# Where the jump of a loop falls: VectorE's loop body rotated in a two-layer graph attention kernel

## What is computed

```python
# layer 0: masked attention, residual, layer norm
q, k, v = heads(x @ Wq + bq), heads(x @ Wk + bk), heads(x @ Wv + bv)
attn = softmax(where(adj == 0, -inf, q @ k.T / sqrt(32)))
x = layernorm((attn @ v) @ Wo + bo + x) * gamma + beta
# layer 1: pre-norm attention with an edge bias, then an MLP
nx = layernorm(x) * g1 + b1
bias = where(adj > 0, 0.1 * adj * adj, -inf)
x1 = x + softmax(q(nx) @ k(nx).T / sqrt(32) + bias) @ v(nx) @ wo + bo
return x1 + gelu((layernorm(x1) * g2 + b2) @ w1 + c1) @ w2 + c2
```

## Time and profile before

| | |
|---|---|
| median of 3 runs | 2272.08 us (2271.01 to 2278.83) |
| profiled execution | 2272.97 us, span 2271.2 us |
| TensorE busy | 2150.3 us, 95% |
| VectorE busy | 1827.5 us, 80% |
| ScalarE busy | 1821.7 us, 80% |
| GpSimd busy | 1238.3 us, 55% |
| DMA, data / code | 10.4% / 0.4% of 16 engines |
| granted TensorE clock, mean | 0.988 |

### The profile page before, as it was taken

The page is one execution under the profiler, slowest core; times in us unless marked ns, Lnnn a source line. Parts: engine busy times, 40 slices in busy tenths (PEclk is TensorE's granted clock), DMA queues, the critical chain, the costliest instruction groups (busy, mean ns, idle before and its releaser), DMA issues.

```text
span 2271.2 us, 59215 instructions
## 1 busy us (share of the span) xinstructions
PE 2150.3 (95%) x19008; PEld 1894.4 (83%) x19008; DVE 1827.5 (80%) x7173; ACT 1821.7 (80%) x5774; POOL 1238.3 (55%) x909
## 2 busy tenths in 40 slices
PE   6889999999999999999999999999999999999997
PEld 5678888888888888888888888888888888888886
DVE  5788888888877888878888878888788887788863
ACT  4688888888788887878888878887788887888863
POOL 2566556556556556455566455565455565565541
PEclk8999999999999999999999999999999999999998
DMA  4101110101110101100101100101101111100000
GB/s 128 38 20 39 34 39 16 38 28 37 33 38 14 38 28 38 33 26 26 38 28 38 33 24 28 38 28 38 33 14 38 30 36 33 38 14 28 25 11 19
DMA packets 80891, 73.79 MB, mean 32 GB/s; under 512 B 3008, under 2 KB 72256, under 8 KB 80704
## 3 DMA queue, kind: packets, MB, share of 16 engines
q1 hardware_dynamic: 80704, 71.98, 10.4%
HBM read 55.20 MB, written 16.78 MB: 32 GB/s over the span
## 4 chain that ended last, share of the span: by engine, by line
PE 76%; DVE 9%; ACT 8%; issue 5%; POOL 1%; DMA 0%; DVEq 0%; SPq 0%; ACTq 0%; POOLq 0%
PE ps L402 56%; PE ps L384 9%; PE ps L371 6%; ACT pm L521 5%; PE ps L395 4%; DVE actl L738 2%; DVE pm L698 2%; PE ps L413 1%; DVE r L798 1%; DVE hf L751 1%; ACT acth L570 1%; ACT pt L529 1%; ACT acth L580 1%; DVE stats L783 1%; POOL pm L857 0%
## 5 line engine op out<-in xcount | busy, mean ns | idle before, releaser
L521 ACT ACTIVATE pm<-pm,nmax 128x128 f32<-128x128 f32 x2048 | 794.9, 395 | 86.4 <-DVE nmax L698 85.9
L857 POOL TENSOR_TENSOR pm<-pm,rinv 128x512 f32<-128x512 f32 x512 | 526.3, 1044 | 359.4 <-DVE rinv L713 359.4
L698 DVE CUSTOM_DVE_ANT_0 pm<-ps,m 128x128 f32<-128x128 f32 x2048 | 465.7, 284 | 26.8 <-PE ps L384 22.3
L521 ACT ACTIVATION_READ_ACCUMULATOR pm<-pm,nmax 128x1 f32 x2048 | 396.0, 193 | 0.0
L872 POOL TENSOR_TENSOR rstd<-veps,power 128x4 f32<-128x4 f32 x96 | 98.1, 1022 | 479.1 <-DVE veps L791 479.0
L384 PE MATMUL ps<-ident,pm 128*128 128x128 f32 x2048 | 301.2, 278 | 8.7 <-POOL pm L857 7.5
L402 PE MATMUL ps<-w2h,hh 128*128 128x256 f32 x1024 | 289.9, 283 | 3.2 <-DVE hl L805 3.2
L402 PE MATMUL ps<-w2l,hh 128*128 128x256 f32 x1024 | 287.1, 280 | 0.0
L402 PE MATMUL ps<-w2h,hl 128*128 128x256 f32 x1024 | 287.1, 280 | 0.0
L384 PEld LDWEIGHTS ps<-ident,pm 128*128 128x128 f32 x2048 | 237.1, 141 | 46.7 <-POOL pm L857 12.3
L402 PE MATMUL ps<-acth,w1h 128*128 128x512 f32 x512 | 212.1, 414 | 2.6 <-DVE actl L732 1.5
(11 more groups left out here) (148 smaller groups left out, 6291.0 us busy)
## 6 DMA issues: line engine op xcount, KB each, us to landing
xTr<-in_xT SPq DMA_DIRECT2D x32, 512.0 KB, 3.6
xy<-in_x SPq DMA_DIRECT2D x32, 512.0 KB, 4.0
out<-x SPq DMA_DIRECT2D x32, 512.0 KB, 2.9
m<-in_adj SPq DMA_DIRECT2D x32, 256.0 KB, 2.8
a<-in_adj SPq DMA_DIRECT2D x32, 256.0 KB, 4.2
r<-in_wo SPq DMA_DIRECT2D x2, 256.0 KB, 6.2
x<-in_w SPq DMA_DIRECT2D x1, 512.0 KB, 8.9
v<-in_w SPq DMA_DIRECT2D x1, 512.0 KB, 6.9
```

The lines of the kernel that those rows point to most:

```text
L521: last = nc.scalar.activation(pm[:, g % 2, h, :], pm[:, g % 2, h, :], ACT.Exp, bias=nmax[:, g % 2, h:h + 1], scale=-1.0, accum_out=rsum[:, ...
L698: last = nc.vector.tensor_tensor_reduce(out=pm[:, g % 2, h, :], in0=src[:, j * N:(j + 1) * N], in1=m[:, g, :], scale=1.0, scalar=3e38, op0 ...
L857: tt(pm[:, g % 2, hs, :], pm[:, g % 2, hs, :], rinv[:, g % 2, hs].rearrange("p (h a) -> p h a", a=1).to_broadcast([P, HC, N]), ALU.mult).t ...
```

## The change

VectorE's `body(i)` is written as the same cyclic sequence of operations with another first one. The operations from `qk_lo(Y, i - 1, 3)` to the end of the old body now stand at the front, with i - 1 in place of i, and the old beginning, from `x_lo(i, 1)` on, follows them. The body now ends with `mask_scores(X, i, 3, 0)`. In all, VectorE executes the same operations in the same order. No other engine's code is changed. The place of the loop's beginning in VectorE's code, and of its jump in the sequence of work, is another one.

```diff
             def body(i):
-                x_lo(i, 1); norm_stats(0, i - 1); split_h(i - 3, 7); norm_rows(0, i - 1); mask_scores(Y, i - 2, 2, 0)
+                qk_lo(Y, i - 2, 3); mask_scores(X, i - 1, 3, 1); v_out(Y, i - 2, 0); v_out(Y, i - 2, 1)
+                recip(X, i - 1, 3); lo("T2", i - 3, 0); mask_scores(Y, i - 2, 0, 0); lo("T2", i - 3, 1)
...
+                split_h(i - 3, 4); split_h(i - 3, 5); residual("WO0", i - 1, 0); split_h(i - 3, 6); x_lo(i, 0)
+                residual("WO0", i - 1, 1); x_lo(i, 1); norm_stats(0, i - 1); split_h(i - 3, 7); norm_rows(0, i - 1)
...
-                norm_rows(2, i - 2); qk_lo(Y, i - 1, 2); mask_scores(X, i, 3, 0); qk_lo(Y, i - 1, 3)
-                mask_scores(X, i, 3, 1); v_out(Y, i - 1, 0); v_out(Y, i - 1, 1); recip(X, i, 3); lo("T2", i - 2, 0)
...
-                x_lo(i + 1, 0); residual("WO0", i, 1)
+                norm_rows(2, i - 2); qk_lo(Y, i - 1, 2); mask_scores(X, i, 3, 0)
 
             iterate(dve, body, {FIRST: first_weights})
```

More of the change, by code:

```diff
@@ L808, in body @@
             def body(i):
-                x_lo(i, 1); norm_stats(0, i - 1); split_h(i - 3, 7); norm_rows(0, i - 1); mask_scores(Y, i - 2, 2, 0)
[L810 to L814, removed]
+                qk_lo(Y, i - 2, 3); mask_scores(X, i - 1, 3, 1); v_out(Y, i - 2, 0); v_out(Y, i - 2, 1)
+                recip(X, i - 1, 3); lo("T2", i - 3, 0); mask_scores(Y, i - 2, 0, 0); lo("T2", i - 3, 1)
+                out_lo(X, i - 1, 0); flipped(X, i - 1, 2, 1); mask_scores(Y, i - 2, 0, 1); copy_pt(X, i - 1, 2)
+                copy_pt(X, i - 1, 3); flipped(X, i - 1, 3, 0); mask_scores(Y, i - 2, 1, 0); mask0(i)
+                recip(Y, i - 2, 0); split_h(i - 3, 0); split_h(i - 3, 1); flipped(X, i - 1, 3, 1)
+                mask_scores(Y, i - 2, 1, 1); split_h(i - 3, 2); split_h(i - 3, 3); out_lo(X, i - 1, 1)
+                split_h(i - 3, 4); split_h(i - 3, 5); residual("WO0", i - 1, 0); split_h(i - 3, 6); x_lo(i, 0)
+                residual("WO0", i - 1, 1); x_lo(i, 1); norm_stats(0, i - 1); split_h(i - 3, 7); norm_rows(0, i - 1)
+                mask_scores(Y, i - 2, 2, 0); copy_pt(Y, i - 2, 0); qk_lo(X, i, 0); recip(Y, i - 2, 1)
+                flipped(Y, i - 2, 0, 1); mask_scores(Y, i - 2, 2, 1); qk_lo(X, i, 1); residual("MLP2", i - 3, 0)
+                qk_lo(X, i, 2); flipped(Y, i - 2, 1, 0); mask_scores(Y, i - 2, 3, 0); recip(Y, i - 2, 2)
+                flipped(Y, i - 2, 1, 1); mask_scores(Y, i - 2, 3, 1); copy_pt(Y, i - 2, 1); qk_lo(X, i, 3)
+                v_out(X, i, 0); norm_stats(1, i - 1); mask1(i - 1); recip(Y, i - 2, 3); flipped(Y, i - 2, 2, 0)
                 mask_scores(X, i, 0, 0); out_lo(Y, i - 2, 0); flipped(Y, i - 2, 2, 1); mask_scores(X, i, 0, 1)
```

## The result

The changed kernel takes 2214.7 us (median of four runs, 2212.6 to 2216.75) against 2272.08 us of the kernel before; the ratio, by the runs of both on the same chips, is 0.9739, 95% interval 0.9714 to 0.9765. The forecast was 2211 us. The profiled execution took 2215.6 us with a span of 2213.8 us. A fourth run of the kernel before, 2682.22 us, fell in a slower state of the chip and counts nowhere here. The kernel before was run again beside the experiments: its medians there were 2278.1, 2274.8 and 2276.7 us, single runs 2270 to 2294 us. So its 2272.08 us is on the low side; by the ratio the gain is some 59 us.

The account below looks back on a forecast made before the run. PE was held up by VectorE's late `x_lo` write, delayed by the loop's jump. Replacing 1716.7 us of periods by 25 x 66.2 saves 61.7 us from 2272.97, giving 2211 us; 8-in-10 range 2204 to 2226 us.

Parts of the forecast that it names:

- The bound: PE, busy 95% of the span: its one large wait, 62.9 us, is for VectorE's `x_lo` write, late through the loop's jump.
- Why the jump costs: VectorE's loop: its body touches four 8 KB code pieces, so five fetches a period and a jump costing 2.9 us.
- Place in the code: VectorE's new loop body: 0.22 + 2.4 = 2.62 pieces, so three touched, 0.38 to spare; the stall and steady-state fetches vanish.
- What PE gets: PE's loop periods: each falls from 68.40 to the straight-line 66.2 us, 25 x 2.2 = 55 us.
- What the clock gets: Loop periods: four stretches at granted clock 0.50, following PE's waits at jumps, vanish too, worth 6.7 us.
- Ends: Straight-line code before and after the loop: same instructions, priced at nothing, one fetch wait of at most 2.9 us either way.
- The first rival: VectorE's new loop edge: the jump still fetches, PE loses about 2.0 us a period, 2261 us (2268 with clock); chance 0.07.
- The second rival: VectorE's new loop edge: the 2.85 us hole is paid in full every period, 2288 us; chance 0.03.
- The third rival: Loop: the stall vanishes but something else, say ScalarE, is late, at most 0.79 us a period, 20 us, 2231 us; chance 0.04.

Follow-up runs that it names:

- the shifted runs: Changed kernel with 24, 40 or 64 unused semaphore counts added at the head of VectorE's code, moving its loop: 2211.5, 2283.2 and 2251.3 us.
- 64 counts: Changed kernel with 64 unused semaphore counts added at the head of VectorE's code, order of work untouched: 2251.3 us, ratio 0.9892 to the kernel before.
- 40 counts: Changed kernel with 40 unused semaphore counts added at the head of VectorE's code, loop from 1033 to 1348: 2283.2 us.
- 128 counts: Kernel before with 128 unused semaphore counts added at the head of VectorE's code, moved one whole 8 KB piece: 2284.0 us, ratio 1.0032.
- 100: Kernel before with 100 unused semaphore counts added at the head of VectorE's code, loop from 1162 to 1476: 2325.8 us, ratio 1.0212.

## Why the prediction was right, and where it was off

*The bound.* Right: the jump's wait was the one large wait of PE. In its place nothing else came; the next row of PE's waits is 7.1 us, as before, and the one for GpSimd's `pm` went from 7.5 to 6.4 us.

*Why the jump costs.* Right: four pieces with one ahead do not stay, three do, now seen from both sides in VectorE itself, by moving the code alone. That the store holds four 8 KB pieces fits all runs; it is still inferred from what is fetched, not seen.

*Place in the code.* Right in what it was for, three pieces, but with less room than I worked out. I had cut by busy instructions: a beginning at 0.22 of a piece, a length of 2.4, and 0.38 to spare, some 49 instructions. By counting it begins at 0.29 (993 against 956) and is 2.46 long (315 of 128), which leaves 0.25, 32 instructions; the shifted runs put it between 24 and 40.

*What PE gets.* The period was taken as 66.2 us, from straight-line code, and the 25 periods sum to 1654.2 us against 1655.0.

*What the clock gets.* Right: no stretch of 0.50 stands in the steady state, here or in the other profiled kernels without a hole, and the 6.7 us are in the 62.5. Its size is that of one execution: the kernel before took between 2270 and 2294 us over its runs, with a mean granted clock from 0.989 down to 0.978.

*Ends.* This step failed, by 5 us. It was costed at nothing, since the same instructions run there. But the emptying had 27.3 us at the lower clock in place of 13.7; PE was busy 17.8 us in these against 6.7 us, and half of the 11 us more, 5.6, is the most that it could lose; 3.8 us were measured. PE's waits are no longer there than before, 17.7 against 18.3 us. The experiments' profiles had between 13.7 and 20.8 us at the lower clock in the emptying. It varies from profile to profile, and I did not find what sets it.

*The first rival.* Its price was mis-sized, and its path was wrong: it was to reach PE through GpSimd's padding and the scores, and reached it through the bank that `mask_scores` frees for the transposes. I took a hole of 2.2 to 2.4 us at the new edge, for 50 us. With 64 counts it was 1.03 us and 36.6 us in all; with 40 counts, 2.25 us and 68 us. What I had missed is that the price depends on how far the sequencer has run ahead of the engine, and on how many instructions lie in the last piece. The second rival, a new edge worse than the old one (2288 us), came near in its number for a shift of 40 instructions, 2283 us, within some 16 instructions of the shift that is fast. That is luck: it had 2.85 us a period paid in full, and what came was 1.8 us of waits at L413 out of a longer hole, some 12 us of lower clock, and small waits elsewhere. *The third rival* (something else late) did not come: 66.2 us is PE's own work.

The forecast's 2211 us is 3.7 us under the median, inside the range. In the profiled executions the loop gave 0.8 us more than forecast (62.5 against 61.7) and the ends took 5.1 us.

## What to carry to other kernels

When one engine shows an idle time put down to "issue" once per iteration, at the same instruction, look at the loop's jump: count the code fetches of one period. If they are not nothing, move the loop by a few dozen instructions or shorten its body until it touches one piece less, or put the jump where that engine waits for another anyway. And treat a kernel with such a loop as fragile: instructions added anywhere ahead of it move its time by some 2 to 3 per cent, up or down (here 2215 to 2326 us, around 2275, for one order of work), so that an edit elsewhere in the program can be credited with what the alignment did.

## What the runs showed of the hardware

- VectorE's code is fetched in pieces of 8 KB, 128 instructions. In these kernels a loop whose body touches three of them runs without any fetch after its first pass (five placements, bodies of 314 to 356 instructions); one that touches four fetches five pieces in every pass (six placements), and from the jump to the loop's first instruction it is 2.8 to 3.1 us in four of them.
- The worst place is a body that ends a few instructions (here eight) into its fourth piece: 3.4 to 3.65 us. The fetch ahead then starts some 0.5 us before that of the target, which takes longer; that this is the reason is inferred.
- The engine's idle time is shorter than this by what is queued on it: 1.0 us (64 counts), 2.3 (40), 2.4 (the kernel before, and with 128 counts) and 3.0 (100), and no idle time of its own where it waits for PE.
- In the written-out iterations from 171 to 370 us no wait of PE, VectorE, ScalarE or GpSimd is put down to "issue", though code is fetched there. ScalarE's, GpSimd's and SyncE's loops, of 223, 46 and 22 instructions and so of at most three pieces, do not fetch in the steady state: the changed kernel has no such fetch between 390 and 2013 us.
- PE's waits of 2.8 us in each period of 70 us went with 20 stretches of the lower clock (1.2 GHz) in 25 periods, waits of 2.06 us with four, waits of 1.8 us at another place with seven, and waits of 0.85 us with none.
